# Two of four gates of an LSTM recurrence as column matmuls, inputs transposed once a batch, and a rearranged prologue

## The reference, cut to what matters

```
x = x + attention over two keys (a no-op key and one made from cond)
x = x + mixture of experts: shared up/down projection, 8 routed experts, top 2
x = x + (gelu(cond @ W_proj + b) @ W_u + x @ W_e)
x = x + LSTM(x, h0 = cond):
        z = x_t @ Wx + b + h @ Wh              # 4 gates of 256 units
        i, f, o = sigmoid(ai), sigmoid(af), sigmoid(ao);  g = tanh(ag)
        c = f * c + i * g;   h = o * tanh(c)
```

## Time and profile before

| | us |
|---|---|
| median of 3 runs | 2178.57 (2178.53 to 2179.19) |
| profiled execution, its own time | 2179.15 |
| its span in the trace | 2177.4 |
| mean granted clock of TensorE, share of 2.4 GHz | 0.997 |
| the first h of the loop starts at | 61.6 |
| the last h starts at | 2173.9 |
| busy: PE, DVE, ACT, POOL | 93%, 64%, 39%, 54% |

### The profile page before, as it was taken

How to read it: one execution, slowest core, us unless ns; L and a number is a source line. 1 busy time by engine, 2 the same in 40 slices (tenths; PEclk the granted TensorE clock), 3 DMA queues, 4 the chain that set the end, 5 groups by cost and what they waited for, 6 DMA issues and landing times. The chain is left out here.

```text
span 2177.4 us, 200920 instructions
## 1 busy us (share of the span) xinstructions
PE 2023.9 (93%) x86306; PEld 1496.4 (69%) x86306; DVE 1402.4 (64%) x7602; ACT 854.8 (39%) x4761; POOL 1173.9 (54%) x5082
## 2 busy tenths in 40 slices
PE   6899999999999999999999999999999999999998
PEld 4666667666766666766676666676667666667666
DVE  1566666666666666666666666666666666666666
ACT  1334343443443434344343343434434334343443
POOL 4455555555555555555555555555555555555555
PEclk8999999999999999999999999999999999999999
DMA  3000000000000000000000000000000000000000
GB/s 149 5 3 4 3 3 3 3 3 3 3 3 3 4 3 3 3 3 3 3 3 3 3 4 3 3 3 3 3 3 3 3 3 4 3 3 3 3 3 3
DMA packets 57581, 14.54 MB, mean 7 GB/s; under 512 B 56161, under 2 KB 56161, under 8 KB 57058
## 3 DMA queue, kind: packets, MB, share of 16 engines
q1 hardware_dynamic: 57570, 14.39, 2.9%
HBM read 12.26 MB, written 2.10 MB: 7 GB/s over the span
## 5 line engine op out<-in xcount | busy, mean ns | idle before, releaser
L887 PEld LDWEIGHTS bank<-wh_sb,h_ring 128*2 128x2 f32 (+2 forms) x65536 | 922.5, 94 | 496.8 <-DVE h_ring L707 481.8
L887 PE MATMUL bank<-wh_sb,h_ring 128*2 128x64 f32 (+2 forms) x65536 | 1107.7, 219 | 92.3 <-DVE h_ring L707 23.6
L680 DVE STREAM_TRANSPOSE bank<-bank 128x64 f32<-128x64 f32 x1024 | 271.9, 266 | 357.8 <-PE bank L887 341.6
L514 ACT ACTIVATE f_act<-bank 128x4 f32<-128x4 f32 x1024 | 177.8, 174 | 812.0 <-DVE bank L680 812.0
L682 DVE STREAM_TRANSPOSE bank<-bank 128x64 f32<-128x64 f32 x1024 | 272.0, 266 | 185.9 <-PE bank L887 185.9
L517 ACT ACTIVATE bank<-bank 128x8 f32<-128x8 f32 x1024 | 165.9, 162 | 280.2 <-DVE bank L682 280.2
L759 PE MATMUL bank<-up_sb,x 128*32 128x512 f32 x2080 | 273.9, 599 | 0.7 <-ACT fall L471 0.7
L688 DVE STREAM_TRANSPOSE bank<-bank 128x64 f32<-128x64 f32 x1024 | 271.9, 266 | 0.7 <-PE bank L887 0.7
L765 PE MATMUL bank<-down_e,hid_t 128*16 128x256 f32 x3096 | 266.0, 379 | 0.0
L707 DVE SCALAR_TENSOR_TENSOR h_ring<-o_act,bank 128x4 f32<-128x4 f32 x1024 | 163.3, 159 | 142.0 <-ACT bank L523 95.0
L375 POOL TENSOR_TENSOR num<-one,fall 128x8 f32<-128x8 f32 x130 | 26.3, 202 | 378.8 <-ACT fall L471 378.8
(11 more groups left out here) (132 smaller groups left out, 2646.8 us busy)
## 6 DMA issues: line engine op xcount, KB each, us to landing
x_a<-in_x SPq DMA_DIRECT2D x129, 16.0 KB, 1.6
x_s<-in_x SPq DMA_DIRECT2D x129, 16.0 KB, 1.7
up_sb<-in_up SPq DMA_DIRECT2D x1, 2048.0 KB, 9.5
out_y<-y_sb SPq DMA_DIRECT2D x128, 16.0 KB, 1.4
down_sb<-in_down SPq DMA_DIRECT2D x1, 1536.0 KB, 13.2
wx_sb<-in_wx SPq DMA_DIRECT2D x1, 1024.0 KB, 14.7
wh_sb<-in_wh SPq DMA_DIRECT2D x1, 1024.0 KB, 16.9
wkv_sb<-in_wkv SPq DMA_DIRECT2D x1, 512.0 KB, 4.7
```

The costliest lines, as they stand in the source:

```text
L514: nc.scalar.activation(f_act[:, :].rearrange("p (c b) -> p c b", b=B), t_f_b[:, :, u * B:(u + 1) * B], ACT.Tanh).then_inc(a_f, 1)
L680: nc.vector.transpose(bank[3][:, 0:HC], z_f_b[:, 0:HC]).then_inc(t_f, 1)
L887: last = nc.tensor.matmul(z[32 * j:32 * j + row + B, 0:HC], h_ring[:, prev, c, WIN - B - row:WIN], wh_v[:, c, g, j, :], start=False, stop= ...
```

## The change

- **Candidate and output** no longer have h as the stationary side. `recur_column` makes 32-unit blocks of Wh (32 columns) the stationary side and moves the two columns of h: for each of two blocks m per group, two contraction halves and four groups j, a matmul of 32 x 2. The result has units on partitions, as the cell wants it; `by_row` names its columns. ACT reads candidate and output from their banks without a transpose, the candidate in an operation of its own. **f and i** stay as they were (`recur_row`), i with a bank and a transpose of its own.
- **The input's share** of candidate and output is made with 128 moving columns for both gates (`inject_x`, u = 6), and turned once a batch by two DVE transposes at the start of u = 0; PE waits for `x_turned` ahead of the candidate of u = 0.
- **The bias** is no longer a matmul with ones: DVE copies it into the banks (`bias_x` u = 5, `bias_f` and `bias_i` u = 7), and the injection adds to it. `padded` and POOL's copy into it are gone, and so is the matmul of cond's term in the third layer: `layer3` adds `cond_t`.
- **Waits and small moves:** DVE's reciprocal of s goes from behind the scan of u = 3 to the start of u = 4; the two waits ahead of h in u = 0, of POOL ahead of `y_sb`, of PE in u = 1 and of DVE ahead of `layer3` change places.
- **Prologue:** the first two batches go through attention and router together, folding begins right behind them and is cut in three parts, `we` and `down` are loaded ahead of `up`, the scaling of Wx, Wh and bias goes to DVE, and fewer banks are cleared.

The diff, cut to its core:

```
-        z_f_b, z_gi_b, z_o_b = bank[0], bank[1], bank[2]
...
+
+        z_f, z_i = bank[0][:, 0:HC], bank[1][:, 0:HC]
+        t_f = bank[6][:, 4 * HC:5 * HC]
+        t_i = bank[1][:, HC:2 * HC]
+        z_x = bank[2][:, HC:3 * HC]
+        z_c, z_o = bank[2][:, 0:HC], bank[3][:, 0:HC]
+
+        def by_row(ap):
+            return ap.rearrange("p (c r) -> p c r", r=32)
+
...
+                    step = slice(u * B, (u + 1) * B)
+                    act.wait_ge(f_turned, now)
                     nc.scalar.activation(f_act[:, :].rearrange("p (c b) -> p c b", b=B),
-                                         t_f_b[:, :, u * B:(u + 1) * B], ACT.Tanh).then_inc(a_f, 1)
-                    act.wait_ge(t_gi, now)
-                    nc.scalar.activation(gi_out.rearrange("p g (c b) -> p g c b", b=B),
-                                         t_gi_b[:, :, :, gi:gi + B], ACT.Tanh).then_inc(terms_in, 1)
-                    act.wait_ge(t_o, now)
+                                         by_row(t_f)[:, :, step], ACT.Tanh).then_inc(a_f, 1)
+                    act.wait_ge(c_made, now)
+                    nc.scalar.activation(factor_q[:, :, 2].rearrange("p (c b) -> p c b", b=B),
+                                         by_row(z_c)[:, :, step], ACT.Tanh)
+                    act.wait_ge(i_turned, now)
+                    nc.scalar.activation(factor_q[:, :, 1].rearrange("p (c b) -> p c b", b=B),
+                                         by_row(t_i)[:, :, step], ACT.Tanh).then_inc(terms_in, 1)
+                    act.wait_ge(o_made, now)
                     nc.scalar.activation(o_act[:, :].rearrange("p (c b) -> p c b", b=B),
-                                         t_o_b[:, :, u * B:(u + 1) * B], ACT.Tanh)
+                                         by_row(z_o)[:, :, step], ACT.Tanh)
                     act.wait_ge(cell, now)
                     nc.scalar.activation(c_tanh, cell_c, ACT.Tanh).then_inc(cell_tanh, 1)
                     if u == 2:
...
+                nc.vector.tensor_tensor(x3[:, :, NB:2 * NB].rearrange("p c (u b) -> p c u b", b=B),
+                                        x3_b.rearrange("p c (u b) -> p c u b", b=B),
+                                        cond_t[:, :, :].unsqueeze(2).to_broadcast([P, C, U, B]),
+                                        ALU.add).then_inc(x3_out, up_to)
+
+
+            def bias_f(up_to):
+                nc.vector.tensor_copy(z_f, bias_sb[:, GF, :]).then_inc(f_bias, up_to)
+
+            def bias_i(up_to):
+                nc.vector.tensor_copy(z_i, bias_sb[:, GI, :]).then_inc(i_bias, up_to)
+
+            def bias_x(up_to):
+                nc.vector.tensor_copy(z_x.rearrange("p (g m) -> p g m", g=2),
+                                      bias_sb[:, GO:GC + 1, :]).then_inc(x_bias, up_to)
...
-                    if u == 1:
+                    if u == 0:
+
+                        dve.wait_ge(x_injected, now)
+                        nc.vector.transpose(z_c, z_x[:, HC:2 * HC])
+                        nc.vector.transpose(z_o, z_x[:, 0:HC]).then_inc(x_turned, U)
+                    elif u == 1:
                         dve.wait_ge(x_ready, now)
...
                     elif u == 4:
+                        invert_s(now)
+                        dve.wait_ge(x3_made, now)
                         dve.wait_ge(moved, now)
-                        dve.wait_ge(x3_made, now)
                         layer3(U)
...
-                    dve.wait_ge(z_f, now)
-                    nc.vector.transpose(bank[3][:, 0:HC], z_f_b[:, 0:HC]).then_inc(t_f, 1)
-                    dve.wait_ge(z_gi, now)
-                    nc.vector.transpose(bank[4][:, 0:HC], z_gi_b[:, 0:HC]).then_inc(t_gi, 1)
+                    dve.wait_ge(f_made, now)
+                    nc.vector.transpose(t_f, z_f).then_inc(f_turned, 1)
+                    dve.wait_ge(i_made, now)
+                    nc.vector.transpose(t_i, z_i).then_inc(i_turned, 1)
+                    if u == 7:
+                        dve.wait_ge(f_turned, now)
+                        bias_f(U)
...
-                    dve.wait_ge(z_o, now)
-                    nc.vector.transpose(bank[3][:, HC:2 * HC], z_o_b[:, 0:HC]).then_inc(t_o, 1)
                     dve.wait_ge(terms_in, dve.snap(t * 2 + (2 * u + 2)))
                     nc.vector.tensor_tensor_scan(cell_all, addend[:, :], factor, 0.0, ALU.add, ALU.mult).then_inc(cell, 1)
-                    if u == 0:
-
-                        dve.wait_ge(h_read, now)
-                    elif u == 1:
+                    if u == 1:
...
-                        invert_s(now)
+                    elif u == 5:
+                        bias_x(U)
                     elif u == 6:
                         hidden_a(now)
                     elif u == 7:
+                        bias_i(U)
                         dve.wait_ge(hid_s_out, now)
                         turn(0, hid_s[:, :], hid_st, U)
                     dve.wait_ge(cell_tanh, now)
+                    if u == 0:
+
+                        dve.wait_ge(h_read, now)
...
-            def inject(z, g, rows, src, const, first):
-
-                for c in range(C + 1):
+
+            def inject(z, g):
+
+                for c in range(C):
                     for j in range(J):
-                        last = nc.tensor.matmul(z[32 * j:32 * j + rows, 0:HC], src[:, c, :] if c < C else const,
-                                                wx_v[:, c, g, j, :] if c < C else bias_v[:, g, j, :],
-                                                start=(first and c == 0), stop=False, skip_group_check=True)
+                        last = nc.tensor.matmul(z[32 * j:32 * j + NB, :], x3[:, c, NB:2 * NB], wx_v[:, c, g, j, :],
+                                                start=False, stop=False, skip_group_check=True)
                 return last
 
-            def inject_fo(z, g):
-                return inject(z, g, NB, x3[:, :, NB:2 * NB], ones[:, 16:32], True)
-
-            def inject_gi():
-
-                inject(z_gi_b, GC, 32, padded[:, :, :], ones, True)
-                return inject(z_gi_b, GI, NB, padded[:, :, NB:2 * NB], ones[:, 16:32], False)
+            def inject_x():
+                for c in range(C):
+                    for j in range(J):
+                        last = nc.tensor.matmul(z_x[32 * j:32 * j + NB, :].rearrange("p (g m) -> p g m", g=2),
+                                                x3[:, c, NB:2 * NB], wx_v[:, c, GO:GC + 1, j, :],
+                                                start=False, stop=False, skip_group_check=True)
+                return last
 
             pe.wait_ge(w_in["wproj"], 16)
...
+            def fold(k):
+
                 if k >= len(FOLD):
                     pe.wait_ge(fold_out, k - len(FOLD) + 1)
                 for c in range(C):
                     last = nc.tensor.matmul(bank[FOLD[k % len(FOLD)]][:, 0:D], down_sb[:, c, k, :], we_sb[:, c, :],
                                             start=(c == 0), stop=(c == C - 1))
                 last.then_inc(fold_made, 1)
-            pe.wait_ge(cond_done, 1)
...
+            def recur_row(z, g, row, prev):
                 for c in range(C):
                     for j in range(J):
-                        last = nc.tensor.matmul(z[32 * j:32 * j + row + B, 0:HC],
+                        last = nc.tensor.matmul(z[32 * j:32 * j + row + B, :],
                                                 h_ring[:, prev, c, WIN - B - row:WIN], wh_v[:, c, g, j, :],
                                                 start=False, stop=(c == C - 1), skip_group_check=True)
                 return last
 
+            def recur_column(z, g, row, prev):
+
+                for m in range(C):
+                    for c in range(C):
+                        for j in range(J):
+                            last = nc.tensor.matmul(by_row(z)[32 * j:32 * (j + 1), m, row:row + B],
+                                                    wh_v[:, c, g, j, 32 * m:32 * (m + 1)],
+                                                    h_ring[:, prev, c, WIN - B:WIN],
+                                                    start=False, stop=(c == C - 1), skip_group_check=True)
+                return last
+
             with nc.Fori(READY, READY + T, U, engines=(PE_ENGINE,), head_slot={PE_ENGINE: 0}) as t:
                 for u in range(U):
...
                     pe.wait_ge(hid, now)
-                    recur(z_f_b, GF, u * B, prev).then_inc(z_f, 1)
-                    recur(z_gi_b, GI, gi, prev)
-                    recur(z_gi_b, GC, 16 + gi, prev).then_inc(z_gi, 1)
-                    recur(z_o_b, GO, u * B, prev).then_inc(z_o, 1)
+                    recur_row(z_f, GF, u * B, prev).then_inc(f_made, 1)
+                    recur_row(z_i, GI, u * B, prev).then_inc(i_made, 1)
                     if u == 0:
+                        pe.wait_ge(x_turned, now)
+                    recur_column(z_c, GC, u * B, prev).then_inc(c_made, 1)
```

(19 more changed lines are left out.)

340 lines of the change are left out of this document (166 added, 174 removed).

## The result

| | before | after |
|---|---|---|
| median, us | 2178.62 | 2077.88 (2075.86 to 2078.56) |
| ratio | | 0.9536, 95% interval 0.9519 to 0.9552 |
| span of the profiled execution, us | 2177.4 | 2074.1 |
| first h starts, us | 61.6 | 46.8 |
| one step, mean over 1023, us | 2.065 | 1.978 |

What follows compares the result with a forecast made beforehand. One chain per step, h to h, bounds the kernel: 0.22 us less per step, after losses 1.49 us per batch, 190 us, plus 10 in the prologue. From 2179.15 that gives 1979, 1978 as median; range 1925 to 2105.

Steps and rivals of the forecast that it cites:

- wrong if: Signs: 32 short records over 0.35 us, scan released by candidate, PE streaming when h comes, steps 0, 2, 4, 5.
- rival 1: Short column records go at about 10 ns, step 1.88 us, 2098 us with the prologue; 15%.
- What bounds the kernel: One chain per step, h, matmuls, transpose, tanh, scan, tanh, h: 2.065 us a step, 97% of the time.
- Price of a column record: Candidate and output matmuls of 2 moving columns start 7.4 ns apart, upper end 13.7; each lasts 0.17 us.
- PE's other work: In steps 0, 2, 4, 5, streams of 0.86 us end at 1.84, next step wants PE at 1.88: fits, barely.
- Steps 2 and 4: Switches between whole-array and 32-column weights after steps 1 and 3 cost 0.10 and 0.20 us per batch.
- Step 0: Two new transposes ahead of f's cost 0.03 us per batch; the other order of two waits gives 0.07 back.
- Step 7: Bias copies, inject, hidden transpose and h queue on DVE: h at 1.70 for 1.67, 0.03 us per batch.
- Prologue: Folding starts earlier and fills PE's idle time: 10 us less, range 5 to 13; loop near 48 or 53.
- Rival 2: Short records no faster than 13.7 ns, 2282 us; extreme of one per 30 ns, about 3300 us; together 8%.
- Rivals 3 and 4: 3: PE's loop outgrows instruction memory, 2267 us, 4%; 4: PE's clock falls to 1.2 GHz, all cold 2900 us, 4%.
- Rival 5: POOL or DVE late: gate chain's 0.2 us margin short, up to 0.3 per batch, 2017 us; 6%.

Runs made afterwards that it cites:

- half candidate: Changed kernel with the second half of the candidate's contraction left out and half of the output gate's made twice; 2069.53 us, ratio 0.9505.
- the square: Four kernels: two activations with up in full 2077.9 us, with half of up's columns 2091.1; one activation for candidate and i 2061.4 and 2053.5.
- one activation: Changed kernel with one ACT operation for candidate and i together in place of two; 2061.35 us, ratio 0.9467.
- attend in step 6: Changed kernel with the two whole-array matmuls of the attention's context moved from step 3 to step 6; 2077.06 us, ratio 0.9536.
- attend in tiles: Changed kernel with step 3's attention context matmuls cut into 32-column tiles; profiled 2052.10 us, median 2111; with one activation and bias of i early, 2031.25.
- early bias of i: Changed kernel with i's tanh ahead of the candidate's and DVE's bias of i ahead of the scan in step 7; 2065.44 us, ratio 0.9486.

## Why the prediction was right, and where it missed

The sign and the range were right, and so was the mechanism in its outline: one chain per step, shortened by taking two gates out of the transposes. The size was forecast twice too large, and the link that comes last was named wrong: the forecast had the transpose of i, the runs show the candidate. Two of the signs that the prediction had set itself as "wrong if" came true. The scan hangs on the candidate (the profile names i's tanh as its releaser, but that tanh had only stood in ACT's queue behind the candidate's), and PE is still at work when h comes: it starts steps 5 and 6 at 0.068, not 0.055. A third did not: 32 records start within 0.28 us, not over 0.35. So that the time fell inside the range is in part luck: the range was wide enough for most of rival 1, whose case this nearly was. By the prediction's own steps:

- *What bounds the kernel.* Right: the chain h, PE, transpose, tanh, scan, tanh, h. The two transposes came where the forecast put them (0.54 and 0.77 for 0.53 and 0.76), so did f's tanh (0.84 for 0.83) and the keep product (1.05 for 1.04).
- *Price of a column record*, **the term that was mis-sized**: 9.1 ns for 7.4. The duration of one was 0.17 us, as forecast. The forecast took a burst of four scores per tile for a steady rate. The candidate's last record starts at 0.790, not 0.72, and the signal from its end to ACT takes 0.097 (1.058 - 0.790 - 0.171), not the 0.07 of a transpose on DVE. So its tanh starts at 1.06, not 0.96; i's comes 0.07 behind it at 1.13, not at 1.06; the scan at 1.32 for 1.25; h ends at 1.89 for 1.83. This is 0.064 x 8 = 0.51 us per batch, x 128 = 65 us. The price alone doesn't make it: put into the forecast's own sum, 9.1 ns gives 0.49 + 31 x 0.0091 + 0.17 + 0.07 = 1.01 for the candidate's tanh and 1.08 for i's. The rest of the way to 1.13 is that the records begin at 0.514, not 0.49 (0.02), and the longer signal (0.03). The margin of 0.03 us for the candidate was named with its condition, 8 ns per record, and the condition failed. That the candidate sets the scan is shown in step 7 of the half candidate.
- *PE's other work* "fits, barely" at 1.84 of 1.88: with records of 9.1 ns it doesn't, since 63 x 0.0017 = 0.11 us are added to PE's load. It is 1.893 for the step, as the square shows. The same price thus stands twice in the result, once in the chain and once in PE's load, and each of the two limits gives 1.89 by itself; a forecast that corrects only one of them promises too much from removing the other, as those for the half candidate and the one activation did.
- *Steps 2 and 4*: 0.10 and 0.20 forecast; 0.14 and 0.23 over a normal step measured. The mechanism for step 4, attend's whole-array matmuls, is shown by the traces of attend in step 6 and of attend in tiles. For step 2 no run settles it. 0.07 a batch, 9 us.
- *Step 0*, **the step that failed**: the price of 0.03 for the transposes of x looked at the wrong engine. The 0.07 for the order of the two waits did come: DVE's idle time before h in step 0 reads 0.23 above, where it read 0.29. But PE's back edge, the way from the end of the loop's body to its start, hidden before, became bare, since the injection of i in step 7 was now the last thing behind a late bias: beside the 0.06 of every step, step 0 misses its forecast by 0.22 us (2.145 - 1.86 - 0.064), 28 us per run. The early bias of i took 0.19 of it away; 0.03 stays, since the transposes of x make the candidate start at 0.675 there, not at 0.55. The prediction had looked for it as "no idle PE by issue at the loop's end" and priced nothing.
- *Step 7*: 0.03 forecast, none found, 4 us to the good.
- *Prologue*: 14.8 us for 10, above the range of 5 to 13. PE kept its clock up to 42.5 us, nearly the more hopeful of the two cases. But the loop was then entered at a lower clock. From the steps' lengths (16.50 - 15.77) x 128 = 93 us were to come, and the loop as a whole became 88.7 shorter: some 5 us were lost at its start, which the forecast had not.
- *Rivals.* Rival 1 (10 ns per record, 2098 us, step 1.88) was nearer than the main case: the truth lay between the two, in the price and in the time. Rival 2 didn't come, 9.1 being under its 11.5. Rivals 3 and 4 are absent from the changed kernel and present in its neighbours: 84 more instructions in the loop brought the refetch at a price of 7.6 us a batch ((3046 - 2078)/128, the lower clock included), over three times the 2.25 us that the prediction gave it, and in the kernels with half of up's columns the lower clock came. Rival 5 did not show: step 7 is as long as step 5.

The pieces: 65 (record price and signal) + 28 (step 0: 24 back edge, 4 transposes) + 9 (switches) - 4 (step 7) = 98 us in the steps, + 5 at the loop's start, - 5 for the prologue, + 2 for the profiled execution being under the median: the 100 us between forecast and result.

## What to carry to other kernels

When several limits of a step lie within a few per cent of each other, price them all with the same uncertain number before summing: here one record price moved the chain and the engine's load at once, and half the gain was gone. Put work on TensorE's queue in whole rounds of its tiles, and look at what stood hidden behind the work that you move: a back edge costs nothing until it is last. Before adding instructions to a loop that just fits, or taking work from a busy TensorE, look at the instruction packets and the granted clock of the result, since either can cost more than the edit brings.

## What the runs showed of the hardware that was not expected

- Weight loads of 32 columns with matmuls of 2 moving columns, spread over four tiles, start 9.1 ns apart over 64 records. In one place they went faster: in step 0 with the bias of i early, where the candidate's records waited for the transposes of x, the same 64 took 0.542 us instead of 0.575. Why was not tried.
- Two whole-array matmuls between tiled ones keep the tiled ones out for 0.53 to 0.55 us, and the eight tiled ones that do the same work for 0.21.
- PE's loop of 1780 weight loads and matmuls was not fetched anew in the two profiled executions that had it (9 packets), one of 1840 was (577).
- The clock fell from 2.4 to 1.2 GHz for 3.4 us at a time in a loop in which PE was busy for 90% and more of every 2 us, when half of the long matmuls' columns were taken away: in 14 batches of one kernel and 6 of the other. In the trace of the changed kernel, with all of them, it did not fall between 63 us and the end of the last step; but executions with attend in tiles, which also make all of them, read mean clocks down to 0.877.
